# A decoder's recurrent products in 32 bits, four instead of twelve

## What is computed

```python
def step(carry, xw):                      # h, c: [16, 128]; U: [128, 512]; 1024 steps
    h, c = carry
    z = xw + h @ U
    i, f, g, o = jnp.split(z, 4, axis=-1)
    i, f, g, o = sigmoid(i), sigmoid(f), tanh(g), sigmoid(o)
    c = f * c + i * g
    h = o * jnp.tanh(c)
    return ((h, c), h)
rep = jnp.broadcast_to(latent[:, None, :], (x.shape[0], x.shape[1], 2 * H))
dec = _lstm(rep @ Wd + bd, Ud, return_sequences=True)
return dec @ Wo + bo                      # then h + this, and the experts on each token
```

## Time and profile before

| | |
|---|---|
| median of three runs | 3900.97 us |
| the profiled execution | 3894.48 us |
| its span, first to last instruction | 3892.7 us |
| TensorE matmuls busy | 3752.8 us, 61839 of them |
| TensorE weight loads busy | 2740.7 us |
| VectorE busy | 3054.7 us |
| ScalarE busy | 2367.2 us |
| mean granted TensorE clock | 0.992 of full |

### The profile page before, as it was taken

The page is one execution under the profiler, slowest core; times in us unless marked ns, Lnnn a source line. Parts: engine busy times, 40 slices in busy tenths (PEclk is TensorE's granted clock), DMA queues, the critical chain, the costliest instruction groups (busy, mean ns, idle before and its releaser), DMA issues. The chain is left out here.

```text
span 3892.7 us, 159805 instructions
## 1 busy us (share of the span) xinstructions
PE 3752.8 (96%) x61839; PEld 2740.7 (70%) x61839; DVE 3054.7 (78%) x21227; ACT 2367.2 (61%) x11882; POOL 86.9 (2%) x129
## 2 busy tenths in 40 slices
PE   8898999999999999999999899999999999999998
PEld 3333888888888888888888666666666666666664
DVE  6998899999999999999998666666666666666664
ACT  3232888888888888888888333443334433333433
POOL 5300000000000000000000000000000000000000
PEclk9999999999999999999999999999999999999999
DMA  3110000000000000000000000000000000000000
GB/s 91 22 28 20 3 3 3 3 3 3 3 3 3 3 3 3 3 3 3 3 3 4 4 8 8 6 8 6 8 8 6 8 6 8 8 8 6 6 8 7
DMA packets 49570, 33.99 MB, mean 9 GB/s; under 512 B 37661, under 2 KB 46877, under 8 KB 48806
## 3 DMA queue, kind: packets, MB, share of 16 engines
q1 hardware_dynamic: 48806, 23.77, 2.4%
HBM read 15.37 MB, written 8.39 MB: 6 GB/s over the span
## 5 line engine op out<-in xcount | busy, mean ns | idle before, releaser
L759 PE MATMUL bank<-xs,ident 128*128 128x128 f16 x15490 | 1397.8, 221 | 0.0
L759 PEld LDWEIGHTS bank<-xs,ident 128*128 128x128 f16 x15490 | 994.6, 101 | 256.3 <-issue 230.0
L779 ACT ACTIVATE ifg_cell_dec<-bank 128x48 f32<-128x48 f32 x1024 | 215.3, 210 | 638.3 <-PE bank L771 638.3
L771 PE MATMUL bank<-enc_lo,u_hi 128*128 128x16 f16 x8192 | 529.3, 173 | 0.3 <-DVE enc_lo L830 0.3
L768 PE MATMUL bank<-enc_hi,u_lo 128*128 128x16 f16 x8192 | 527.7, 172 | 0.0
L794 DVE SCALAR_TENSOR_TENSOR terms_dec<-ifg_cell_dec 128x32 f32<-128x32 f32 x1024 | 197.0, 192 | 387.7 <-ACT ifg_cell_dec L779 377.4
L768 PE MATMUL bank<-enc_hi,u_hi 128*128 128x16 f16 x8192 | 499.9, 169 | 0.0
L768 PEld LDWEIGHTS bank<-enc_hi,u_lo 128*128 128x128 f16 x8192 | 339.2, 96 | 205.6 <-DVE enc_hi L824 171.1
L786 ACT ACTIVATE bank<-bank 128x16 f32<-128x16 f32 x1024 | 172.0, 168 | 411.7 <-DVE bank L800 411.7
L771 PEld LDWEIGHTS bank<-enc_lo,u_hi 128*128 128x128 f16 x8192 | 339.3, 96 | 68.6 <-DVE enc_lo L830 0.4
L768 PEld LDWEIGHTS bank<-enc_hi,u_hi 128*128 128x128 f16 x8192 | 349.7, 96 | 0.0
(11 more groups left out here) (268 smaller groups left out, 7932.1 us busy)
## 6 DMA issues: line engine op xcount, KB each, us to landing
g_rows<-tok_d_gamma_batched_dram SPq DMA_DIRECT2D x8, 512.0 KB, 6.5
x_rows<-in_x_dram SPq DMA_DIRECT2D x16, 256.0 KB, 3.1
kept_h<-tok_ln_h SPq DMA_DIRECT2D x32, 128.0 KB, 2.1
res<-kept_h SPq DMA_DIRECT2D x32, 128.0 KB
out_dram<-sums SPq DMA_DIRECT2D x32, 128.0 KB
raw_wd<-in_L_attn_Wd_dram SPq DMA_DIRECT2D x2, 256.0 KB
raw_experts<-in_L_ffn_W_dram SPq DMA_DIRECT2D x2, 256.0 KB
raw_u<-in_L_attn_Uf_dram SPq DMA_DIRECT2D x1, 256.0 KB
```

What stands on the lines that cost most here:

```text
L759: nc.tensor.matmul(spare, m.ident16[:], m.xs[:, 0, :, :].rearrange("p b t -> p (b t)"), start=False, stop=True, skip_group_check=True)
L771: last = nc.tensor.matmul(z[k], m.u_hi[c.d][:, g, :], h_lo, start=False, stop=True, skip_group_check=True)
L779: nc.scalar.activation(c.ifg_cell[:, 0:3, :], ifg, ACT.Tanh, scale=1.0 / Z_SCALE).then_inc(c.s_t_ifg, 1)
```

## The change

The recurrent weights of the decoder are kept in 32 bits (the third of the raw arrays, scaled in place as before, now lives on as `u_dec`). `pe_gates_full` replaces `pe_gates` in the decoder's body: it waits for c.h alone and makes one 32-bit product for each gate. VectorE makes c.h first and the high part behind it, and waits for the high part before it makes the low part. Both parts are still made in each step, for the projection. The encoder keeps `pe_gates` and `dve_hidden` as they are, and so do idle products, fills and expert parts.

```diff
--- before.py
+++ after.py
@@ -142,10 +142,11 @@
         m.enc_hi = [sb(f"enc_hi{d}", [P, B], F16) for d in range(2)]
         m.enc_lo = [sb(f"enc_lo{d}", [P, B], F16) for d in range(2)]
 
+        m.u_dec = sb("u_dec", [P, 4 * H], F32)
         raw_ctx, raw_sb, raw_sem = tools(nc)
         with raw_ctx:
 
-            m.raw_u = [raw_sb(f"raw_u{d}", [P, 4 * H], F32) for d in range(3)]
+            m.raw_u = [raw_sb(f"raw_u{d}", [P, 4 * H], F32) for d in range(2)] + [m.u_dec]
             m.raw_w = [raw_sb(f"raw_w{d}", [P, 4 * H], F32) for d in range(2)]
             m.raw_wd = [raw_sb(f"raw_wd{d}", [P, 4 * H], F32) for d in range(2)]
             m.raw_wo = raw_sb("raw_wo", [P, D], F32)
@@ -774,6 +775,18 @@
     last.then_inc(c.s_z_o, 1)
 
 
+def pe_gates_full(nc, pe, m, c, n, ifg, o):
+
+    z = (ifg[:, 0, :], ifg[:, 1, :], ifg[:, 2, :], o)
+    pe.wait_ge(c.s_h, n + 1)
+    for k, g in enumerate(SLOT_GATE):
+        at = GATE_FROM[g] * H
+        last = nc.tensor.matmul(z[k], m.u_dec[:, at:at + H], c.h[:], start=False, stop=True, skip_group_check=True)
+        if g == G_:
+            last.then_inc(c.s_z_ifg, 1)
+    last.then_inc(c.s_z_o, 1)
+
+
 def act_gates(nc, act, c, n, ifg, o):
     act.wait_ge(c.s_z_ifg, n + 1)
     nc.scalar.activation(c.ifg_cell[:, 0:3, :], ifg, ACT.Tanh, scale=1.0 / Z_SCALE).then_inc(c.s_t_ifg, 1)
@@ -823,6 +836,13 @@
     tt = nc.vector.tensor_tensor
     tt(h_hi, c.out_gate[:], c.tanh_cell, ALU.mult).then_inc(c.s_hi, 1)
     tt(c.h[:], c.out_gate[:], c.tanh_cell, ALU.mult).then_inc(c.s_h, 1)
+
+
+def dve_hidden_full(nc, c, h_hi):
+
+    tt = nc.vector.tensor_tensor
+    tt(c.h[:], c.out_gate[:], c.tanh_cell, ALU.mult).then_inc(c.s_h, 1)
+    tt(h_hi, c.out_gate[:], c.tanh_cell, ALU.mult).then_inc(c.s_hi, 1)
 
 
 def dve_hidden_low(nc, dve, c, n, h_hi, h_lo):
@@ -1177,7 +1197,7 @@
                     for step in range(BODY):
                         q, s = divmod(step, STEPS)
                         n = BODY * i + step
-                        pe_gates(nc, pe, m, c, n, h_at(ring_hi, n - 1), h_at(ring_lo, n - 1), *at(step))
+                        pe_gates_full(nc, pe, m, c, n, *at(step))
                         if s in (1, 3, 5):
                             fill((q + 1) % 2, s // 2)
                         for j, start in tiles:
@@ -1238,6 +1258,7 @@
                 V.memset(sums[:], 0.0).then_inc(s_out, 1)
                 V.memset(h_at(ring_hi, -1), 0.0).then_inc(c.s_hi, 1)
                 V.memset(h_at(ring_lo, -1), 0.0).then_inc(c.s_lo, 1)
+                V.memset(c.h[:], 0.0).then_inc(c.s_h, 1)
                 dve.wait_ge(s_given, 1)
                 own.link(V.tensor_copy(given[:], m.bank[4][:, 0:4 * B]))
                 third = parts[:].rearrange("p k g b -> p k (g b)")
@@ -1381,9 +1402,11 @@
                         part(in_tanh, tiles, step)
                         dve.wait_ge(c.s_tanh_cell, n + 1)
                         dve.wait_ge(c.s_out_gate, n + 1)
-                        dve_hidden(nc, dve, c, n, h_at(ring_hi, n))
+                        dve_hidden_full(nc, c, h_at(ring_hi, n))
                         dve_half_cell(nc, dve, c, n + 1)
-                        dve_hidden_low(nc, dve, c, n, h_at(ring_hi, n), h_at(ring_lo, n))
+                        dve.wait_ge(c.s_hi, n + 2)
+                        nc.vector.tensor_tensor(h_at(ring_lo, n), c.h[:], h_at(ring_hi, n), ALU.subtract
+                                                ).then_inc(c.s_lo, 1)
                         part(in_gates, tiles, step)
 
                 bodies(dve, body)
```

## The result

The changed kernel takes 5982.69 us (median of four, 5981.9 to 5983.3) against 3900.27 us for the kernel before: a ratio of 1.534, interval 1.531 to 1.536, 2082 us more. The sign was right and the size was not: 4292 us was forecast, 4195 to 4375 as the range.

What follows compares the result with a forecast made beforehand. It took the decoder as bound by a chain through three engines beside TensorE's queue. Empty, middle and full places added 2.7, 2.7 and 6.9 us a body: 382 over 31 bodies, plus 10, +392, 4292 us (range 4195 to 4375).

Steps and rivals of the forecast that it cites:

- The block at full clock: TensorE's products of h: eight loads 0.109 us apart hold it 0.87 us instead of 0.38; L779 0.87 behind the first.
- The chain's +0.30: Dependent work of a decoder step, from h's products through ScalarE's gates: 0.30 us longer a step.
- The queue: TensorE's work before the next h: block +0.49 us; middle places +0.34 a step, full places +0.46, empty ones only +0.30.
- Nothing from the order on VectorE: VectorE's four operations between h and low part, issued in another order: low part keeps its place, no cost.
- rival 2: TensorE, a gap of 0.09 us at each return to fp16: 4360 us, or 4435 with gaps on both sides; chance 0.12.
- Rival 3: Decoder's light steps: TensorE's granted clock falls for stretches of 7 us in each body, put at 4450 us; chance 0.08.
- Rival 1: Decoder steps: filler work gives way and only the chain's +0.30 us a step is paid, 4208 us; chance 0.13.
- rivals 4 and 5: h products: 4, loads at fp16's 0.025 spacing, 3690 us, chance 0.03; 5, a second pair of loads per product, 4880-5200, 0.01.

Runs made afterwards that it cites:

- The stand-in in fp16: The kernel before with 19 more narrow fp16 products that nobody reads inside the block of h, idle products unchanged: 4447.18 us, ratio 1.140.
- the kernel with the redundant wait: The kernel before with VectorE's order of the change and a second wait, for c.h, in front of the low part: 3980.72 us, ratio 1.022.
- the three filled kernels: The changed kernel with 96 entry idle products and more in light places (5460.19 us); also none in full places (5494.57); fewer light places, more in 0 to 2 (4754.99).

## Why the prediction was wrong

- **The block at full clock: right.** Eight loads, two a product, 0.111 apart at full clock (0.109 forecast). The rule of the Trainium skill that names four passes ("FP8 and Floating Point Precision", TensorE Precision Notes) does not show as four loads: each product has two here as well, 8192 for 4096. L792 starts 0.88 behind the first load (0.87 forecast).
- **The chain's +0.30: right.** +0.31 in light steps (1.99 against 1.68).
- **The queue: right, a little small.** 2.14 to 2.24 in full places (2.145 forecast), 2.02 to 2.06 in middle ones (2.02). In sum +420, added up from measured steps, against +392.
- **Nothing from the order on VectorE: right** (ratio 1.0001). Gaps between fp16 and 32-bit products of one shape (rival 2): none; behind the block's first load the next kind's comes 0.81 later (2145.62 and 2146.43), 0.03 behind the start of the last of eight, less than one spacing of 0.111.
- **The clock: wrong, and this is the step that failed.** Rival 3 had the mechanism's first half, with 0.08, and the wrong size. I argued from the encoder's 1.00 over 1737 us and from the 10 or 13 idle products that stay in the light steps, and did not ask of each light step how much of it they would still fill when it is 1.99 and not 1.68 us long. The stand-in in fp16, at 2.05, and the kernel with the redundant wait, at 1.75, both lose the clock without any new 32-bit product. The measured decoder was at 0.50 for all of its 3808 us, where the sum had it at full clock. And I priced a fall as a stretch of 7 us that ends, as the one in the earlier trace rows does. I had put the doubled load at 0.8 us more a block in the same paragraph (measured 8 x (0.214 - 0.111) = 0.82), but priced neither the other work of the step at the lower clock, nor asked if the fall would end: the steps take 3.0 to 4.2 us and the fall does not end. This kernel's own idle products thus did not keep the clock at steps of 2.0 to 2.2 us, and did not regain it at steps of 3.0 to 4.2 us in 3808 us.

Shown: the lower clock is present for all of the 3808 us; the block runs at either level; full clock with enough idle products gives 4788; fp16 products in a slightly longer step lose the clock and get it back; and more idle products in the light places can bring it back with the 32-bit block in place. The split of the 2082 us into about 420 at full clock and about 1660 for the clock is an estimate that rests on summed places. Open: why the stand-in leaves the lower clock with 13 and 10 idle products and the changed kernel does not. Its steps there are shorter, at most 3.05 us against 3.0 to 3.75 in the same places, 6 to 9, and have no 32-bit block, and no run parts the two. Why the falls of the three filled kernels lie in places 2, 6, 8, 19, 20, 25 and 30 is not shown by any run here either.

Rival 1 (chain only) fell with the full places' 2.17, rivals 4 and 5 with the loads' count and spacing.

## What to carry to other kernels

Where filler keeps a clock up, it is sized for a step's length: work out anew, for each step, how much of it is filled once the step is longer, before a clock seen elsewhere in the trace is taken over. Price both levels in full, with every term at the lower one, and ask if the kernel could get out of the lower one again (here it did not, in 3808 us; with six more idle products in the light places it did, in about half of the bodies). The busy share in the records doesn't answer that: TensorE counts as busy for 3805 of those 3808 us at 0.50. And count loads, not products: four products of 32 bits were eight loads of 0.11 us in place of twelve of 0.025.

## What the runs showed that was not expected

- The same places of the body take 2.0 to 2.2 us at one clock and 3.0 to 4.2 at the other, and a kernel with 9712 more products is 1194 us faster (4788 against 5983).
- Half clock costs fp16 products of 16 columns little: 0.026 us a load against 0.025, and +130 us for a decoder at a mean clock of 0.63 without idle products.
- A second wait ahead of one VectorE operation in the chain, on something already done, moved it by 0.07 us and the kernel by 83 us, and cost some of its clock.
